# Cross-attention and FP4 FFN on one core: semaphores for the leading stack rows, and another placement of prologue, quantization and late-normalisation work

## The chip, the core and the metric

The kernel runs on one core of a Trainium2 chip. The core has TensorE (PE, with PEld its weight load), VectorE (DVE), ScalarE (ACT), GpSimd (POOL), and SyncE (SP), which here only issues DMAs. An engine's name with a q, as ACTq, is its sequencer, which waits and issues DMAs. The metric is device time in microseconds, the median of several executions; lower is better.

## What is computed

Eight batches of `x` (512 rows of 256) attend to a context of 1601 rows of 256, with 16 heads of 16; then comes a feed-forward part with blockwise FP4 quantization of activations and weights.

```python
x = x + xattn(layernorm(x), ctx, ctx, Wq, bq, Wk, bk, Wv, bv, Wo, bo)
# xattn: softmax(q k^T / 4) v per head, then @ Wo.T + bo
x = x + ffn(layernorm(x), w_gate, w_up, w_down)
# ffn: h = silu(fp4(x) @ fp4(w_gate).T) * (fp4(x) @ fp4(w_up).T); fp4(h) @ fp4(w_down).T
# fp4: per block of 16, scale = max|.|/6, values rounded to the grid 0 .5 1 1.5 2 3 4 6
```

## The kernel before, in words

The kernel is a software pipeline over batches. Iterations are called pre (the prologue), first, six of kind loop, last and tail. In a loop iteration four parts run together: attention of one batch ("att"), the projections of the next ("early"), layernorm and loads of the one after ("next"), and output projection and FFN of the previous one ("late"). The first iteration has no late part, but quantizes and transposes the FFN weights instead ("once"). The last one has no early part.

An iteration has 52 steps: four groups of four heads times 13 tiles of the context. A step does, in this order on TensorE: the scores of two heads (L678), a job from the first list of `SLOTS`, the scores of the other two heads, two products for the row maxima (L692, 26 a group, 18 steps ahead of the scores; in the first steps of the first iteration three), a job from the second list, and the weighted sum of the step before (L707). ScalarE does four exps (L870) and takes most jobs' results; VectorE reduces the products (L941, L943) and runs the pieces of layernorm and quantization that `DVE_EXTRA` and `W_SCALE_AT`, `W_POWER_AT` place behind them; GpSimd does what `POOL_WORK` places. Every engine runs its list in order, and waits in order. Jobs share one bank of PSUM (three in the prologue), so a job waits until its predecessor's result was taken. Products alternate between two buffers.

Queries and keys are split into three bf16 parts, written to DRAM, and read back into `qstack` and `kstack`, whose rows are blocks of parts: 48 leading rows in each half, which the products read, made from two arrangements of the parts. Each half of a group takes six transfers from the queries and six from the keys, and all twelve of a kind count on one semaphore, `q_stack[g]` or `k_stack[g]`. Rows 32 to 63 of the stacks are filled by GpSimd (L1190, L1191) before the transfers: group 0 first, the rest after the first layernorm is ready. Once a group's products are reduced, the negated maxima are transposed (job nm), split on VectorE (L989 to L992) and written by three transfers (L396) as a row of `qstack` that the scores need.

In the prologue, ScalarE issues the query transfers of group 0 (L862), waits for all of them, then loads the other weights. Products of group 0 start at step 34. Job q1 is at step 35, the second half of the keys at 36 to 39, eight v jobs in pairs at 40, 42, 44 and 46. At step 45 TensorE computes the bias that comes from bv and Wo (L735); VectorE adds it to `bob` and clears the bank. At step 47 ScalarE issues the first two raw FFN weight loads (L760).

The weight quantization of one of six pieces: VectorE takes maxima and scales (L1135 to L1137), GpSimd scales (L1249), VectorE makes powers (L1146, L1147), GpSimd rounds in three instructions (L1255 to L1259), and two wT jobs transpose it (L653).

## Time and profile before

| what | value |
|---|---|
| median of 3 runs | 1815.83 us (1815.01 to 1816.35) |
| profiled execution, its own time | 1818.33 us |
| its span, first to last instruction | 1816.5 us |
| PE, DVE, ACT, POOL busy | 1693.3, 1364.4, 1152.6, 522.3 us |
| mean granted TensorE clock | 0.975 |

Spans are cut at the first exp of an iteration or of a step. Instruction groups stand with their line in the kernel, and an arrow `<-` goes from what is written to what is read.

### The profile page before, as it was taken

What the parts mean: (1) busy time and instruction counts of PE and PEld (TensorE: products, weight loads), DVE (VectorE), ACT (ScalarE), POOL (GpSimd) and SP (SyncE); (2) the same over time, 40 slices, a digit from 0 to 9 for tenths busy, and PEclk for the clock granted to TensorE, in tenths of its full rate; (3) what the DMA queues carried; (4) which work ended last, traced back from release to release, by engine and by line L of the source; (5) the groups of instructions that cost most, each with busy time, mean ns of one, the idle gap of its engine ahead of it and who ended that gap; (6) DMA issues with size and microseconds to landing.
All of it is one profiled execution on the core that took longest, in us unless ns stands there. A gap on an engine that the chain in (4) does not pass through costs nothing.

```text
span 1816.5 us, 26586 instructions
## 1 busy us (share of the span) xinstructions
PE 1693.3 (93%) x9600; PEld 662.7 (36%) x9600; DVE 1364.4 (75%) x1970; ACT 1152.6 (63%) x2335; POOL 522.3 (29%) x409
## 2 busy tenths in 40 slices
PE   2699779999999999999999999999999999989978
PEld 2332113433343334433443334433334333323335
DVE  4677778688778877688777887688877887688538
ACT  2167557776667666676667766676667766656651
POOL 4306432153203422062302531054211532012203
PEclk8899889999999999999999999999999999999989
DMA  5544305142240424233060324215051421300000
GB/s 142 143 68 95 59 29 110 19 102 40 75 74 30 88 39 97 36 69 73 25 123 28 75 40 100 48 43 99 19 115 16 102 40 41 60 1 1 10 15 12
DMA packets 98030, 109.08 MB, mean 60 GB/s; under 512 B 18788, under 2 KB 83308, under 8 KB 97900
## 3 DMA queue, kind: packets, MB, share of 16 engines
q1 hardware_dynamic: 93344, 103.26, 27.5%
q10 hardware_dynamic: 4556, 4.13, 0.9%
q8 instruction: 76, 1.25, 0.3%
q14 instruction: 54, 0.44, 0.1%
HBM read 76.78 MB, written 30.16 MB: 59 GB/s over the span
## 4 chain that ended last, share of the span: by engine, by line
PE 75%; DVE 15%; ACT 4%; issue 2%; DMA 1%; POOL 1%; ACTq 0%; SPq 0%; DVEq 0%; POOLq 0%
PE pvb L707 19%; PE st L678 19%; PE mx L692 10%; DVE cmx L941 7%; PE misc L629 7%; PE misc L591 4%; ACT prob L870 3%; PE misc L584 3%; PE misc L646 3%; PE misc L641 2%; PE misc L523 1%; PE misc L608 1%; PE misc L637 1%; PE misc L561 1%; PE misc L572 1%
## 5 line engine op out<-in xcount | busy, mean ns | idle before, releaser
L870 ACT ACTIVATE prob<-st 128x512 f32<-128x512 f32 x1630 | 885.9, 598 | 432.8 <-PE st L678 431.1
L941 DVE TENSOR_REDUCE cmx<-mx 128x2 f32<-128x1024 f32 x768 | 905.9, 1219 | 263.0 <-PE mx L692 259.2
L678 PE MATMUL st<-qstack,kstack 112*128 112x512 bf16 x1630 | 520.9, 388 | 32.5 <-ACT prob L870 17.1
L707 PE MATMUL pvb<-prob,vv 128*17 128x512 f32 (+1 forms) x3328 | 443.4, 605 | 0.6 <-ACT prob L870 0.6
L678 PEld LDWEIGHTS st<-qstack,kstack 112*128 112x128 bf16 x1630 | 128.3, 98 | 552.9 <-issue 293.8
L692 PE MATMUL mx<-kstack,qstack 48*128 48x512 bf16 (+1 forms) x2048 | 253.5, 337 | 43.7 <-DMA qstack<-scr_q 21.3
L1203 POOL TENSOR_TENSOR cin<-cin 128x400 f32<-128x400 f32 (+1 forms) x60 | 55.4, 923 | 374.8 <-ACT cin L798 374.8
L1236 POOL TENSOR_TENSOR ht<-ht,rh 128x704 f32<-128x704 f32 x29 | 40.2, 1388 | 414.6 <-DVE rh L917 414.6
L629 PE MATMUL misc<-wguT,rowsT 128*128 128x352 f32 x456 | 154.3, 460 | 0.0
L692 PEld LDWEIGHTS mx<-kstack,qstack 48*128 48x128 bf16 x2048 | 57.5, 94 | 207.3 <-issue 154.8
L591 PE MATMUL misc<-wv,ctxT 128*128 128x256 f32 (+1 forms) x392 | 102.6, 384 | 0.0
L629 PEld LDWEIGHTS misc<-wguT,rowsT 128*128 128x128 f32 x456 | 86.8, 191 | 40.5 <-issue 0.9
L707 PEld LDWEIGHTS pvb<-prob,vv 128*17 128x17 f32 (+1 forms) x3328 | 55.2, 95 | 116.9 <-issue 95.1
L584 PE MATMUL misc<-ctxT,wk 128*128 128x400 f32 (+1 forms) x240 | 90.8, 500 | 0.0
L591 PEld LDWEIGHTS misc<-wv,ctxT 128*128 128x128 f32 (+1 forms) x392 | 73.7, 188 | 20.5 <-issue 0.5
L1216 POOL TENSOR_TENSOR x<-x,bob 128x1024 f32<-128x1024 f32 x8 | 18.9, 2366 | 193.5 <-DMA x<-x 193.5
L1240 POOL TENSOR_TENSOR ht<-ht,mt 128x704 f32<-128x704 f32 x30 | 50.4, 1680 | 60.2 <-DVE mt L1117 60.2
L1205 POOL TENSOR_TENSOR cin<-cin,one 128x400 bf16<-128x400 f32 (+1 forms) x60 | 57.6, 960 | 4.7
L1207 POOL TENSOR_TENSOR cin<-cin 128x400 bf16<-128x400 f32 (+1 forms) x60 | 55.9, 932 | 4.7
L943 DVE TENSOR_REDUCE cmx<-mx 128x8 f32<-128x520 f32 x64 | 44.4, 693 | 15.6 <-PE mx L692 15.6
L584 PEld LDWEIGHTS misc<-ctxT,wk 128*128 128x128 f32 x240 | 45.4, 190 | 25.0 <-issue 0.7
L973 DVE SCALAR_TENSOR_TENSOR ht<-misc,ht 128x352 f32<-128x352 f32 x57 | 29.7, 520 | 31.9 <-PE misc L629 31.7
(202 smaller groups left out, 1564.5 us busy)
## 6 DMA issues: line engine op xcount, KB each, us to landing
kstack<-scr_k SPq DMA_DIRECT2D x384, 100.1 KB, 4.4
scr_k<-cin SPq DMA_DIRECT2D x48, 300.0 KB, 3.9
qstack<-scr_q SPq DMA_DIRECT2D x372, 32.0 KB, 2.5
cin<-ctx_in SPq DMA_DIRECT2D x8, 1280.0 KB, 7.1
scr_q<-qp SPq DMA_DIRECT2D x15, 384.0 KB, 4.7
scr_k<-cin SPq DMA_DIRECT2D x16, 300.8 KB, 4.5
xn<-x SPq DMA_DIRECT2D x8, 512.0 KB, 4.0
x<-x SPq DMA_DIRECT2D x8, 512.0 KB, 3.8
```

Of the source, the lines that this page charges most:

```text
L584: last = mm(o[:, 0:w], wk[:, h, m * 128:(m + 1) * 128], ctxT[:, h, COFF[n]:COFF[n] + w], start=(h == 0), stop=(h == NC2 - 1))
L591: last = mm(o[0:w, 0:E], ctxT[:, h, KOFF[j]:KOFF[j] + w], wv[:, h, :], start=(h == 0), stop=(h == NC2 - 1))
L629: last = mm(o[:, 0:IH], rowsT[:, h, t * 128:(t + 1) * 128], wguT[:, h, first:first + IH], start=(h == 0), stop=(h == NC2 - 1))
L646: last = mm(o[:, 0:E], hqT[0:FW[f], f, :], wdT[0:FW[f], f, :], start=(f == 0), stop=(f == NF - 1))
L678: mm(score_bank(it, n, pair, h)[0:KROWS[kt], :], kstack[:, hd, KOFF[kt]:KOFF[kt] + KROWS[kt]], qstack[:, hd, :], start=True, stop=True).th ...
L692: last = mm(mx[:, q % 2, par, at:at + w], qstack[r0:r0 + LEAD, hd, t * 128:(t + 1) * 128], kstack[r0:r0 + LEAD, hd, k0:k0 + w], start=True ...
L707: last = mm(pvb[32 * h:32 * h + D + 1, :], vv[0:w, kt, HG * g + h, :], prob[0:w, n % 2, h, :], start=(kt == 0), stop=(kt == NKT - 1))
L870: activate(prob[0:KROWS[kt], n % 2, 2 * pair + h, :], score_bank(it, n, pair, h)[0:KROWS[kt], :], ACT.Exp, scale=SCALE).then_inc(exp_done[ ...
L941: v.tensor_reduce(cmx[:, g % 2, h0:h0 + 2, at:at + 1], products, op=ALU.max, axis=AX.X).then_inc(max_free, 1)
L1203: g_.tensor_tensor(whole, whole, parts[:, 0, :], ALU.subtract).then_inc(step, 1)
L1205: g_.tensor_tensor(parts[:, 1, :], whole, one[:, 0:1].to_broadcast([128, whole.shape[-1]]), ALU.mult).then_inc(step, 1)
L1207: g_.tensor_tensor(parts[:, 2, :], whole, parts[:, 1, :], ALU.subtract).then_inc(done, 1)
```

## The change

The six first transfers of a group, now those with the leading rows of both halves, count on a semaphore of their own; products wait for these, scores for all. In the prologue q1 moves to step 34, keys to 35 to 38, one v job a step from 39 to 46; the fill of the other heads' rows moves behind the first query split, the bias product becomes a job "bob" of the first iteration's step 20, and the raw weight loads move to its step 4. Weight pieces and their transposes get other steps. In the other iterations the second half of the keys is done by step 19, the next context is loaded sooner, gate, up and down jobs shift, and the late normalisation's pieces get steps of their own (the multiplication of `xscale` becomes `xmul`). A down job's first part waits for the first copy of its input alone.

```diff
@@ -83,40 +82,40 @@
     13: ([("k", 3, "early")], []),
     14: ([("k", 4, "early")], []),
     15: ([("q", 1, "early")], []),
-    16: ([("pvT", 0, "att")], [("xqT", 0, "late")]),
-    17: ([("k", 5, "early")], [("xqT", 1, "late")]),
-    18: ([("k", 6, "early")], []),
-    19: ([("gate", 0, "late")], []),
-    20: ([("gate", 1, "late")], []),
-    21: ([("up", 0, "late")], [("nm", 2, "att")]),
-    22: ([("up", 1, "late"), ("wT", 0, "once")], []),
-    23: ([("gate", 2, "late"), ("wT", 1, "once")], []),
-    24: ([("gate", 3, "late"), ("wT", 2, "once")], []),
-    25: ([("up", 2, "late"), ("wT", 3, "once")], []),
-    26: ([("up", 3, "late")], [("hqT", 0, "late")]),
-    27: ([("gate", 4, "late")], [("hqT", 1, "late")]),
-    28: ([("down0", 0, "late")], []),
-    29: ([("down", 0, "late")], [("pvT", 1, "att")]),
-    30: ([("gate", 5, "late")], []),
-    31: ([("up", 4, "late"), ("wT", 4, "once")], [("hqT", 2, "late")]),
-    32: ([("up", 5, "late"), ("wT", 5, "once")], [("hqT", 3, "late")]),
-    33: ([("gate", 6, "late"), ("wT", 6, "once")], []),
-    34: ([("down0", 1, "late")], []),
-    35: ([("down", 1, "late")], [("nm", 3, "att")]),
-    36: ([("gate", 7, "late"), ("wT", 7, "once")], []),
-    37: ([("up", 6, "late")], [("hqT", 4, "late")]),
-    38: ([("up", 7, "late")], [("hqT", 5, "late")]),
-    39: ([("down0", 2, "late")], []),
-    40: ([("down", 2, "late"), ("wT", 8, "once")], []),
-    41: ([("k", 7, "early")], []),
-    42: ([("v", 0, "early")], [("pvT", 2, "att")]),
-    43: ([("v", 1, "early")], [("hqT", 6, "late"), ("wT", 9, "once")]),
-    44: ([("v", 2, "early")], [("hqT", 7, "late")]),
-    45: ([("down0", 3, "late"), ("wT", 10, "once")], []),
-    46: ([("down", 3, "late"), ("wT", 11, "once")], []),
+    16: ([("k", 5, "early")], []),
+    17: ([("k", 6, "early")], []),
+    18: ([("pvT", 0, "att")], [("xqT", 0, "late")]),
+    19: ([("k", 7, "early")], [("xqT", 1, "late")]),
+    20: ([("gate", 0, "late"), ("bob", 0, "once")], []),
+    21: ([("gate", 1, "late")], [("nm", 2, "att")]),
+    22: ([("up", 0, "late")], []),
+    23: ([("up", 1, "late")], []),
+    24: ([("gate", 2, "late"), ("wT", 0, "once")], []),
+    25: ([("gate", 3, "late"), ("wT", 1, "once")], []),
+    26: ([("up", 2, "late")], []),
+    27: ([("up", 3, "late"), ("wT", 2, "once")], [("hqT", 0, "late")]),
+    28: ([("gate", 4, "late"), ("wT", 3, "once")], [("hqT", 1, "late")]),
+    29: ([("down0", 0, "late")], []),
+    30: ([("down", 0, "late")], []),
+    31: ([("gate", 5, "late")], [("pvT", 1, "att")]),
+    32: ([("up", 4, "late")], [("hqT", 2, "late")]),
+    33: ([("up", 5, "late")], [("hqT", 3, "late")]),
+    34: ([("gate", 6, "late"), ("wT", 4, "once")], [("nm", 3, "att")]),
+    35: ([("down0", 1, "late"), ("wT", 5, "once")], []),
+    36: ([("down", 1, "late")], []),
+    37: ([("gate", 7, "late"), ("wT", 6, "once")], [("hqT", 4, "late")]),
+    38: ([("up", 6, "late"), ("wT", 7, "once")], [("hqT", 5, "late")]),
+    39: ([("up", 7, "late")], []),
+    40: ([("down0", 2, "late")], []),
+    41: ([("down", 2, "late")], [("pvT", 2, "att")]),
+    42: ([("v", 0, "early")], []),
+    43: ([("v", 1, "early")], [("hqT", 6, "late"), ("wT", 8, "once")]),
+    44: ([("v", 2, "early")], [("hqT", 7, "late"), ("wT", 9, "once")]),
+    45: ([("down0", 3, "late")], []),
+    46: ([("down", 3, "late")], []),
     47: ([("v", 3, "early")], [("nm", 0, "early")]),
-    48: ([("v", 4, "early")], []),
-    49: ([("v", 5, "early")], []),
+    48: ([("v", 4, "early")], [("wT", 10, "once")]),
+    49: ([("v", 5, "early")], [("wT", 11, "once")]),
     50: ([("v", 6, "early")], []),
     51: ([("v", 7, "early")], []),
...
-    35: ([("q", 1, "early")], []),
-    36: ([("k", 4, "early")], []), 37: ([("k", 5, "early")], []), 38: ([("k", 6, "early")], []), 39: ([("k", 7, "early")], []),
-    40: ([("v", 0, "early"), ("v", 1, "early")], []), 42: ([("v", 2, "early"), ("v", 3, "early")], []),
-    44: ([("v", 4, "early"), ("v", 5, "early")], []), 46: ([("v", 6, "early"), ("v", 7, "early")], []),
+    34: ([("q", 1, "early")], []),
+    **{35 + j: ([("k", 4 + j, "early")], []) for j in range(4)}, **{39 + j: ([("v", j, "early")], []) for j in range(8)},
...
 DVE_EXTRA = {
-    1: [("late", "norm", 3)], 5: [("late", "stats", 0)], 6: [("late", "stats", 1)], 7: [("late", "mean", 0)],
-    9: [("late", "root", 0)], 10: [("att", "nm", 1), ("late", "apply", 0)], 11: [("late", "apply", 1), ("late", "xmax", 0)],
-    12: [("late", "xscale", 0)], 13: [("late", "xpower", 0)], 15: [("late", "xlast", 0)], 16: [("att", "norm", 0)],
-    21: [("att", "nm", 2)], 22: [("late", "hscale", 0)], 23: [("late", "hpower", 0)], 26: [("late", "hscale", 1)], 27: [("late", "hpower", 1)],
-    29: [("att", "norm", 1)], 32: [("late", "hscale", 2)], 33: [("late", "hpower", 2)], 35: [("att", "nm", 3)], 38: [("late", "hscale", 3)], 39: [("late", "hpower", 3)],
-    42: [("att", "norm", 2), ("next", "stats", 0)], 43: [("next", "stats", 1)], 45: [("next", "mean", 0)], 46: [("next", "root", 0)],
+    1: [("late", "norm", 3)], 5: [("late", "stats", 0)], 6: [("late", "stats", 1)], 7: [("late", "mean", 0)], 8: [("late", "root", 0)],
+    9: [("late", "apply", 0)], 10: [("att", "nm", 1)], 11: [("late", "apply", 1)], 12: [("late", "xmax", 0)], 13: [("late", "xscale", 0)],
+    14: [("late", "xmul", 0)], 15: [("late", "xpower", 0)], 17: [("late", "xlast", 0)], 19: [("att", "norm", 0)],
+    21: [("att", "nm", 2)], 23: [("late", "hscale", 0)], 24: [("late", "hpower", 0)], 27: [("late", "hscale", 1)], 28: [("late", "hpower", 1)],
+    31: [("att", "norm", 1)], 33: [("late", "hscale", 2)], 34: [("late", "hpower", 2)], 35: [("att", "nm", 3)], 39: [("late", "hscale", 3)], 40: [("late", "hpower", 3)],
+    42: [("att", "norm", 2)], 43: [("next", "stats", 0)], 44: [("next", "stats", 1)], 45: [("next", "mean", 0)], 46: [("next", "root", 0)],
     47: [("early", "nm", 0)], 49: [("next", "apply", 0)], 50: [("next", "apply", 1)],
...
-W_SCALE_AT = {17: 0, 18: 1, 26: 2, 29: 3, 35: 4, 39: 5}
-W_POWER_AT = {19: 0, 21: 1, 28: 2, 30: 3, 37: 4, 41: 5}
+W_SCALE_AT = {17: 0, 19: 1, 28: 2, 31: 3, 38: 4, 41: 5}
+W_POWER_AT = {20: 0, 22: 1, 30: 2, 33: 3, 40: 4, 43: 5}
...
-    14: [("late", "xround", 0), ("early", "k", 3)], 15: [("early", "k", 4)], 16: [("early", "q", 1)], 18: [("early", "k", 5)], 19: [("early", "k", 6)],
-    23: [("late", "hscaled", 0)], 24: [("late", "hround", 0)], 27: [("late", "hscaled", 1)], 28: [("late", "hround", 1)],
-    33: [("late", "hscaled", 2)], 34: [("late", "hround", 2)], 39: [("late", "hscaled", 3)], 40: [("late", "hround", 3)], 42: [("early", "k", 7)],
+    14: [("early", "k", 3)], 15: [("early", "k", 4)], 16: [("early", "q", 1), ("late", "xround", 0)], 17: [("early", "k", 5)], 18: [("early", "k", 6)], 20: [("early", "k", 7)],
+    24: [("late", "hscaled", 0)], 25: [("late", "hround", 0)], 28: [("late", "hscaled", 1)], 29: [("late", "hround", 1)],
+    34: [("late", "hscaled", 2)], 35: [("late", "hround", 2)], 40: [("late", "hscaled", 3)], 41: [("late", "hround", 3)],
...
+        k_stack = [[sem(f"k_stack{g}_{n}") for n in ("lead", "rest")] for g in range(NG)]
+        q_stack = [[sem(f"q_stack{g}_{n}") for n in ("lead", "rest")] for g in range(NG)]
...
                 src = scr_q.rearrange("(h i) a n -> i h a n", i=D)
-                for half in range(2):
+                for rest in range(2):
                     for par in range(2):
-                        for j, a in enumerate(Q_PARTS[half ^ par]):
-                            row = HALF * half + D * j
-                            sp.dma_start(qstack[row:row + D, HG * g + par:HG * (g + 1):2, :], src[:, HG * g + par:HG * (g + 1):2, a, :]).then_inc(q_stack[g], 16)
...
 
-                sp.wait_ge(q_stack[0], STACK)
-                sp.wait_ge(k_stack[0], STACK)
+                sp.wait_ge(q_stack[0][0], BLOCKS)
+                sp.wait_ge(k_stack[0][0], BLOCKS)
...
                     queries_in(it, 0, "early")
                     keys_in(it, 0, "early")
+                    keys_out(it, 1, range(1))
                     queries_out(it, 1)
-                    keys_out(it, 1, range(3))
+                    keys_out(it, 1, range(1, 4))
                 if has_att:
                     maxima_in(it, 2, "att")
+                if has_next:
+                    ctx_in_rows(it, "next")
                 if has_early:
                     queries_in(it, 1, "early")
                     keys_in(it, 1, "early")
@@ -495,16 +498,11 @@
                     rows_out(it, 1)
                 if has_next:
                     x_in(it, "next")
-                if has_late:
-                    rows_out(it, 2)
-                if has_early:
-                    keys_out(it, 1, range(3, 4))
-                if has_next:
-                    ctx_in_rows(it, "next")
                 if has_early:
                     queries_in(it, 2, "early")
                     keys_in(it, 2, "early")
                 if has_late:
+                    rows_out(it, 2)
                     rows_out(it, 3)
                 if has_att:
...
+                    elif kind == "bob":
+
+                        pe.wait_ge(bvl_ready, 1)
+                        for h in range(NC2):
+                            last = mm(o[:, 0:E], bvl[:, h, :], wo[:, h, :], start=(h == 0), stop=(h == NC2 - 1))
...
                             last = turn(o[0:FW[f], n * 128:(n + 1) * 128], ht[:, t, f * 128:f * 128 + FW[f]], ident[:, :])
                     elif kind == "down0":
-                        pe.wait_ge(free["hqT"], c(2 * QT, 2 * j + 2))
+                        pe.wait_ge(free["hqT"], c(2 * QT, 2 * j + 1))
                         for f in range(NF // 2):
                             mm(o[:, 0:E], hqT[0:FW[f], f, :], wdT[0:FW[f], f, :], start=(f == 0), stop=False)
                         return
                     elif kind == "down":
-                        pe.wait_ge(free["hqT"], c(2 * QT, 2 * j + 2))
+                        if it.kind == "tail":
+                            pe.wait_ge(free["hqT"], c(2 * QT, 2 * j + 1))
                         for f in range(0 if it.kind == "tail" else NF // 2, NF):
+                            if f == (4 if it.kind == "tail" else NF // 2):
+                                pe.wait_ge(free["hqT"], c(2 * QT, 2 * j + 2))
                             last = mm(o[:, 0:E], hqT[0:FW[f], f, :], wdT[0:FW[f], f, :], start=(f == 0), stop=(f == NF - 1))
                     else:
                         p, half = divmod(j, 2)
...
-                        pe.wait_ge(k_stack[g], it.count(part, STACK, STACK))
-                        pe.wait_ge(q_stack[g], it.count(part, STACK, STACK))
+                        pe.wait_ge(k_stack[g][0], it.count(part, BLOCKS, BLOCKS))
+                        pe.wait_ge(q_stack[g][0], it.count(part, BLOCKS, BLOCKS))
                     need(pe, max_free, it.count(part, M_BATCH, q - 1))
...
-                    if it.kind == "pre" and n == BIAS_AT:
-                        pe.wait_ge(s_ones, 2)
-                        pe.wait_ge(bvl_ready, 1)
-                        for c in range(NC2):
-                            last = mm(pvb[:, 0:E], bvl[:, c, :], wo[:, c, :], start=(c == 0), stop=(c == NC2 - 1))
-                        last.then_inc(bo_full, 1)
-
...
                         first_queries()
-                        act.wait_ge(q_stack[0], STACK)
-                        act.wait_ge(k_stack[0], STACK)
+                        act.wait_ge(q_stack[0][1], BLOCKS)
+                        act.wait_ge(k_stack[0][1], BLOCKS)
                         weights_in()
-                    if it.kind == "pre" and n == 47:
+                    if it.kind == "first" and n == 4:
                         raw_in(0)
                         raw_in(1)
                     if has_att:
...
                         link(below(rx[:, :]), part)
+                    elif what == "xmul":
                         link(v.tensor_tensor(blocks(xa[:, :]), blocks(xa[:, :]), over(rx[:, :]), ALU.mult), part)
...
 
-            for heads, done in ((slice(0, HG), 4), (slice(HG, H), 6)):
-                if done == 6:
-                    pool.wait_ge(xn_ready, 1)
+            def fill(heads, done):
+
                 g_.memset(kstack[32:64, heads, :].bitcast(F32), 1.0 + 2.0 ** -23 * 0x3F80).then_inc(c_link, 1)
                 g_.memset(qstack[32:64, heads, :].bitcast(F32), 0.0).then_inc(c_link, 1)
                 pool.wait_ge(c_link, done)
+
+            fill(slice(0, HG), 4)
 
             def bias_columns():
...
-                    if it.kind == "pre" and n == BIAS_AT:
+                    if it.kind == "pre" and n == 15:
+                        pool.wait_ge(q_split, 1)
+                        fill(slice(HG, H), 6)
+                    if it.kind == "first" and n == 6:
                         bias_columns()
```

Left out: the removed names, the same renaming of `half` to `rest` in `keys_in` and in ScalarE's `first_queries`, and the take of "bob" on VectorE, which adds the product into `bob` and signals `free["bob"]`, which GpSimd's bias step waits for.

## Rows read from the trace of the kernel before

**Rows 1.** The page, part 1: busy us (share of the span) xinstructions.
```profile
PE 1693.3 (93%) x9600; PEld 662.7 (36%) x9600; DVE 1364.4 (75%) x1970; ACT 1152.6 (63%) x2335; POOL 522.3 (29%) x409
```

**Rows 2.** The windows, by iteration: us, then PE, PEld, DVE, ACT, POOL busy, clock.
```profile
0.00:92.44 92.44, 44.44 (x177) 24.49 (x178) 50.89 (x98) 20.19 (x40) 33.24 (x31) 0.80 0.59 141
92.44:313.70 221.26, 192.67 (x1080) 59.87 (x1080) 171.61 (x201) 137.38 (x277) 77.54 (x55) 0.93 0.36 71
313.70:522.42 208.72, 205.79 (x1196) 80.93 (x1195) 163.30 (x237) 143.25 (x291) 60.86 (x50) 1.00 0.30 63
1566.83:1751.14 184.31, 174.94 (x1010) 61.23 (x1008) 115.08 (x171) 124.86 (x252) 31.60 (x19) 0.98 0.08 14
```

**Rows 3.** The windows, single steps and runs of steps, in order.
```profile
216.58:220.05 3.47, 2.84 (x17) 0.55 (x16) 2.79 (x4) 2.16 (x4) 1.49 (x1) 1.00 1.04 136
175.98:206.12 30.14, 20.18 (x101) 4.90 (x101) 23.84 (x23) 12.03 (x25) 18.88 (x11) 0.77 0.10 33
227.59:245.53 17.94, 11.45 (x67) 3.03 (x66) 13.95 (x15) 7.47 (x15) 9.99 (x5) 0.85 0.07 21
256.33:267.07 10.74, 8.39 (x33) 1.38 (x32) 8.78 (x11) 4.32 (x8) 4.28 (x4) 0.70 0.15 52
153.30:156.96 3.66, 3.66 (x27) 1.20 (x26) 2.23 (x3) 3.15 (x7) 2.46 (x4) 1.00 0.30 98
790.42:795.17 4.75, 3.90 (x28) 1.38 (x27) 4.68 (x6) 3.15 (x7) 0.44 (x1) 1.00 0.04 16
1619.77:1625.54 5.77, 4.85 (x23) 0.84 (x22) 5.62 (x7) 2.17 (x6) 1.74 (x1) 0.50 0.01 1
850.53:855.21 4.68, 4.68 (x28) 1.95 (x27) 3.37 (x4) 2.62 (x6) 1.96 (x2) 1.00 0.19 41
```

**Rows 4.** The chain of waits in the prologue: start us, us, what.
```profile
39.88 5.52 DMA qstack<-scr_q
...
46.58 3.18 PE st L572 x4
...
69.47 1.86 PE st L591 x4
...
86.38 5.23 DMA qstack<-nmp
```

**Rows 5.** The timeline, all engines, first key split.
```profile
11.75 8.10 POOL L1190 MEMSET kstack<- 32x9612 f32 x1 [6.53 <-DVE xn L1035]
...
19.60 0.58 DVE L1123 TENSOR_TENSOR cin<-cin 128x401 f32<-128x401 f32 x1 [7.97 <-ACT cin L798]
19.80 2.65 POOL L1191 MEMSET qstack<- 32x3072 f32 x1
...
20.21 2.47 DVE L1125 CAST cin<-cin 128x401 bf16<-128x401 f32 x1
...
23.81 0.37 DVE L1125 CAST cin<-cin 128x400 bf16<-128x400 f32 x1
```

**Rows 6.** The DMA issues from 37.0 to 37.3: KB each, us to landing.
```profile
qstack<-scr_q ACTq DMA_DIRECT2D x2, 32.0 KB, 7.2
```

**Rows 7.** The DMA issues of the whole span, same columns.
```profile
qstack<-nmp SPq DMA_DIRECT2D x96, 4.0 KB, 1.7
```

**Rows 8.** The timeline, first and last reductions, raw weight loads.
```profile
46.19 1.23 DVE L941 TENSOR_REDUCE cmx<-mx 128x2 f32<-128x1024 f32 x1 [11.82 <-PE mx L692]
...
82.91 0.22 DVE L947 TENSOR_REDUCE nmx<-cmx 128x16 f32<-128x64 f32 x1
...
83.69 0.90 ACTq L760 DMA_DIRECT2D ht<-w_gate  x2
```

**Rows 9.** The timeline, split of the maxima at step 21, first iteration.
```profile
190.31 2.34 POOL L1255 TENSOR_TENSOR ht<-ht,mt 88x1024 f32<-88x1024 f32 x1 [1.60 <-DVE mt L1147]
190.39 2.40 DVE L990 TENSOR_TENSOR nmr<-nmf,nmp 16x128 f32<-16x128 f32 x1
```

**Rows 10.** The timeline, TensorE, last down job of the tail.
```profile
1810.91 2.40 PE L646 MATMUL mx<-wdT,hqT 128*128 128x256 f32 x10 [0.86 <-ACT hqT L834]
```

More of the change, by code:

```diff
@@ L857, in first_queries @@
                     src = scr_q.rearrange("(h i) a n -> i h a n", i=D)
[L858 removed]
+                    for rest in range(2):
                         for par in range(2):
[L860 to L862 removed]
+                            for j, a in enumerate(Q_PARTS[rest]):
+                                row = HALF * (par ^ rest) + D * j
+                                act.dma_start(qstack[row:row + D, par:HG:2, :], src[:, par:HG:2, a, :]).then_inc(q_stack[0][rest], 16)
                 def exps(n, pair):
@@ L951, in take @@
                     kind, j, part = job
-                    if kind not in ("o", "gate", "up", "down"):
+                    if kind not in ("o", "gate", "up", "down", "bob"):
                         return
@@ L957, in c @@
                         return it.count(part, per, k)
-                    dve.wait_ge(full[kind], job_count(it, job))
-                    if kind == "o":
+                    dve.wait_ge(full[kind], 1 if part == "once" else job_count(it, job))
+                    if kind == "bob":
+                        v.tensor_tensor(bob[:, :], bob[:, :], src[:, 0:E], ALU.add).then_inc(free["bob"], 1)
+                    elif kind == "o":
                         if j == 0:
```

48 lines of the change are left out of this document (21 added, 27 removed).

## The prediction, made before the changed kernel ran

> **What bounds the kernel now.** I read the busy shares, cut the span into iterations, cut the iterations into steps, then followed the chain of waits where a cut was longer than its neighbours. TensorE is busy 93% of the span [rows 1], but that mixes stages. The six loop iterations take 208.7 us each at full granted clock, TensorE busy 205.8 of them: nearly tight. The prologue before the first exp takes 92.4 us with TensorE busy 44.4. The first iteration takes 221.3 with 192.7 busy, though it has no FFN work [rows 2]. So the slack is in those two.
>
> The step is the unit. A step with no projection job takes 3.47 us, TensorE only 2.84 busy [rows 3]: scores, exp, scores, exp, two products, weighted sum. One job between the two halves of the scores hides under the exps (a v step also takes 3.47); the excess, and any job behind the products, adds to it. VectorE must reduce two products a step, 2.27 us, and the products have two buffers: an extra of up to 2.4 us behind the reductions costs nothing, what exceeds it holds TensorE.
>
> Where steps exceed this: steps 20 to 24 of the first iteration take 30.1 us against 17.6 (4 at 3.47, one at 3.68 with a transpose); steps 31 to 33 take 17.9 against 10.4; steps 37 and 38 take 10.7 against 6.9 [rows 3]: 12.5 + 7.5 + 3.8 = 23.8 us lost around the weight quantization. Step 14 takes 4.75 in a loop iteration but 3.66 in the first, which has no late normalisation; in the last iteration it takes 5.77, at a granted clock of 0.50 [rows 3].
>
> **Prologue, until the first reduction.** The chain passes a VectorE cast of 2.47 us that shares its interval with the GpSimd fill of the stack; the same cast takes 0.37 for the next piece [rows 5]. The fill of the other heads moves behind the first query split, so the first key split ends 2.1 us earlier. Keys out and their stack transfers move by about 2.0; the query's split and write follow ScalarE's third and fourth key pieces, which wait for that split, and move by 1.9 until their own product holds them. Products then wait for stack rows: now for all twelve query transfers, the last of which lands at 39.88 + 5.52 = 45.40 [rows 4]. With the lead semaphore they wait for six. The sixth is issued at 37.03 and takes some 7.2 us [rows 6], so 44.1; less 1.9 to 2.0, 42.1. **Term: 3.3 us.**
>
> The moved fill takes 8.10 + 2.65 us [rows 5], from 29.2 to 40, over VectorE's layernorm of the next batch, and SyncE waits for it before it issues group 1. Both are needed only at 42, so it costs nothing; without that cover, SyncE's wait would delay group 1. A two-input VectorE operation ran its normal 0.58 us under the first fill [rows 5]. The Trainium skill (SBUF — State Buffer, section "SBUF: two separate sides") says two SBUF inputs are held only against a GpSimd operation that reads SBUF, while a two-port mode is held by any; this row agrees, and by that rule the layernorm is free at 32.5. If each small operation were held, it would end at 42.7: 0.6 us worse.
>
> **Prologue, the reductions.** The first starts at 46.19, the last work on them ends at 82.91 + 0.22: 36.9 us [rows 8]. Pure VectorE work is 24 x 1.135 + 2 x 0.65 = 28.5. The rest comes from q1 between the first products (3.18 us at low clock), v jobs in pairs (1.86 and 1.71 at low clock), and the bias product [rows 4]. Now q1 runs before the stack arrives, each step has one job, and the bias is out. I keep 1.4 us for the first key job at low clock, 0.7 for the next, 0.9 for turnarounds: 31.5. **Term: 5.4 us**; bounds 8.4 (VectorE alone) and 2 (only bias and q1 gain).
>
> **Prologue, the row of maxima.** The last of its three transfers lands 5.23 us after issue [rows 4]; the median over the kernel is 1.7 [rows 7]. Two raw weight loads of 352 KB are issued at 83.69, just ahead [rows 8]. They move to step 4 of the first iteration. I take 1.9: **3.3 us**, bounds 0 and 3.6. GpSimd's splits end near 62, keys land at 65, so the next context's load is done near 73, ahead of the row at 76. The first exp moves 12.0 us earlier, to about 80.4.
>
> **First iteration.** VectorE from step 19: reductions 2.27, norm 0.7, scales 2.2; then the bias add 0.42, 2.27, powers 1.4 plus 1.1 of contention; then 2.1, the split of the maxima 1.0 plus contention; then 2.27. That split is the dear one: beside GpSimd's rounding a 0.28 us subtraction took 2.40, as long as GpSimd's 2.34 us instruction [rows 9]. It now starts 2.2 us into a rounding of 6.6, so it is held 4.4 us. Sum 20.1 us over four steps of 14.5: 5.6 lost instead of 12.5, **gain 6.9**. At 31, scale and norm still meet the rounding begun at 30, as they now do at 29: about 4.3 lost, plus 1.4 for low clock; the wait at 33 for a piece to be transposed goes: **gain 1.8**. The last pieces have pauses of two steps: 1 lost of 3.8, **gain 2.8**. Against it: four transposes go behind the products where one was, **+1.6**; two raw loads on ScalarE's queue, **+0.7**. Net 9.2; bounds 3 (contention persists) and 16.
>
> **Loop iterations.** Late apply, maximum, scale, multiply and power get a step each, and no extra is over 2.4 us, so step 14 falls to the first iteration's 3.66 and step 15 rises 0.1: -1.0. The rest is a permutation of the same jobs: a last down job paired with a transpose costs 4.68 where 3.86 + 0.59 would do [rows 3]. Pairing transposes with gate jobs, which are released only after tanh and multiply, costs some 0.15 each; down 2 with a transpose, 0.2; the pairs undone give most of it back: +0.3. Net 0.65 a loop, **4 us in six**; bounds -9 and +4. SyncE now issues the next context's load some 20 steps earlier, behind key pieces written near step 21: hidden, since the next thing behind it is needed near step 26 or later. GpSimd's late rounding now follows q1 and ends near 1.2 us before VectorE asks for it.
>
> **Last iteration and tail.** Steps 11, 13 and 14 return to 3.4 to 3.5: 3.3 us; one gate job moves past step 33, where no product hides it: +1.0. Net **2.3**. In the tail, down jobs wait for both copies of their input, 0.86 us, the last at 1810.91 [rows 10]; with half the wait, 0.35 each for two on the path: **0.7**. Bias and weights-in are otherwise unchanged.
>
> **Sum.** 12.0 + 9.2 + 4 + 2.3 + 0.7 = 28.2 us. The profiled execution took 1818.33 us: 1790.1. The median of the runs is 2.5 us below it: 1787.6, say 1788.
>
> **Rivals.** (a) *Low clock in the prologue.* If TensorE stays at 1.2 GHz through the v jobs (granted 0.5 made them 1.86 us), each step is 1.86 + 0.9 against 2.27, and key jobs 3.6: 6 us more, 1794. For: the clock did fall there. Against: one v a step, without pairs, leaves fewer gaps. (b) *Contention moves but stays.* VectorE and GpSimd do the same quantization work; if the held operations just change names, the first iteration gives 3 or less, 1794 to 1798. For: each rounding is still 6.6 us beside small VectorE operations. Against: the waits for GpSimd itself do go. (c) *Loops gain more.* If late reductions also caused what pairs of jobs cost now, each loop gives 2 us: 1780 or below. (d) *Slower.* GpSimd's late rounding sits behind q1's split, and VectorE waits for it in order, the reductions behind it. It gives slower only if it ends over 7 us later than I place it: 1.2 + 1.2 of slack, then 4.7 us a loop to eat the whole gain; 1825 at 8.5 late. For: one GpSimd operation is stretched by contention now and then. Against: its queue has some 2 us of room a step. (e) *The change doesn't do what it says* at the first products: SyncE or ScalarE could still hold them to the last rows; then 1.3 less, inside the range.
>
> **Chances.** Forecast within 6 us either way 0.5; (a) or (b) or both 0.27, 1794 to 1803; (c) 0.17, 1773 to 1782; (d) 0.03; something unseen 0.03. The range takes in (a), (b) and most of (c): 1775 to 1802. Measurement of this kernel tells about 0.2%, 3.6 us. Faster by more 0.95, within 0.01, slower 0.04.
>
> **What would show it.** First products near 42; 26 reductions without gaps of 2 us, ending near 74; row of maxima landing 2 us after issue; first exp near 80. In the first iteration steps 20 to 24 near 23 to 24 us, step 31 or 33 still long, 37 and 38 at 3.5. Loop iterations near 208.0, with step 14 at 3.7. Wrong it would be if loops moved by over 1.5 us each, or if steps 19 to 23 lost as much as 20 to 24 do now.

## The result, and the profile after

The changed kernel takes 1802.26 us, the median of 4 runs (1801.16 to 1803.74), where the kernel before took 1816.09 beside it (1815.01 to 1821.07). The ratio is 0.9923, its 95% interval 0.9908 to 0.9938: faster by 0.8%, half of the 28 us that I forecast, and just above the range. The profiled execution took 1801.16 us, its span is 1799.4. The page's part 1, against [rows 1]:

```profile
PE 1687.2 (94%) x9600; PEld 658.4 (37%) x9600; DVE 1398.6 (78%) x1969; ACT 1155.4 (64%) x2335; POOL 528.4 (29%) x409
```

VectorE is busy 34 us longer for the same instructions: some of them are held. The windows by iteration, against [rows 2]: prologue, first iteration, first loop iteration, last iteration to the first exp of its step 51. (The window of [rows 2] for the last iteration ends 3.2 us behind that exp, so these two lines don't compare; the table below cuts both alike.)

```profile
0.00:78.74 78.74, 40.84 (x173) 21.31 (x174) 56.30 (x96) 19.90 (x39) 32.98 (x31) 0.85 0.64 154
78.74:291.25 212.51, 190.17 (x1084) 60.72 (x1084) 169.57 (x202) 137.65 (x278) 77.12 (x55) 0.95 0.39 78
291.25:501.66 210.41, 206.52 (x1196) 80.97 (x1195) 168.28 (x237) 143.62 (x290) 61.85 (x49) 1.00 0.30 63
1551.75:1733.00 181.25, 170.54 (x993) 60.45 (x991) 119.75 (x171) 123.41 (x249) 31.56 (x19) 1.00 0.08 15
```

| stretch | before | after | difference | forecast |
|---|---|---|---|---|
| prologue, to the first exp | 92.44 | 78.74 | -13.7 | -12.0 |
| first iteration | 221.26 | 212.51 | -8.8 | -9.2 |
| six loop iterations | 1253.13 | 1260.50 | +7.4 | -4 |
| last iteration, to its step 51 | 181.09 | 181.17 | +0.1 | -2.3 |
| tail, from there to the end | 68.61 | 66.44 | -2.2 | -0.7 |

So the loops have the wrong sign, and are 11 us off; the prologue and the first iteration hold; the last two lines are near the forecast only together. These stretches are those of the two profiled executions, which are 17.2 us apart where the medians are 13.8 apart. The six loop iterations take 210.41, 210.32, 209.87, 210.38, 209.86 and 209.66 us.

The steps of [rows 3] in the windows after: 20 to 24, 31 to 33 and 37 to 38 of the first iteration; step 14 of the first loop iteration and of the last; then steps 31 and 49 of the first loop iteration, which before took 4.27 and 3.47.

```profile
162.94:188.31 25.37, 19.98 (x97) 4.75 (x97) 23.59 (x27) 11.36 (x22) 16.93 (x11) 0.80 0.28 90
209.36:225.75 16.39, 10.65 (x59) 2.56 (x59) 16.15 (x18) 6.96 (x15) 8.57 (x4) 0.80 0.00 1
236.37:243.33 6.96, 6.33 (x41) 1.84 (x39) 4.71 (x5) 4.83 (x10) 0.00 (x0) 1.00 0.48 140
350.58:354.24 3.66, 3.66 (x27) 1.20 (x26) 3.13 (x6) 3.16 (x7) 2.52 (x4) 1.00 0.28 93
1604.22:1607.61 3.39, 2.62 (x22) 0.65 (x22) 3.18 (x6) 2.18 (x5) 0.00 (x0) 1.00 0.03 7
418.25:422.79 4.54, 4.33 (x26) 1.73 (x25) 3.41 (x4) 2.98 (x8) 0.00 (x0) 1.00 0.00 0
490.02:494.70 4.68, 3.71 (x22) 1.39 (x21) 4.61 (x7) 2.39 (x6) 0.00 (x0) 1.00 0.02 3
```

Step 14 is what I said it would be. Step 49 isn't: TensorE is busy 3.71 of 4.68 us and VectorE 4.61. The timeline of VectorE, GpSimd and the products ahead of it shows why:

```profile
487.27 2.37 POOL L1215 TENSOR_TENSOR x<-x,bob 128x1024 f32<-128x1024 f32 x1 [21.71 <-DMA x<-x]
487.42 2.29 DVE L991 CAST nmp<-nmf 16x128 bf16<-16x128 f32 x1
...
490.51 4.60 DVE L941 TENSOR_REDUCE cmx<-mx 128x2 f32<-128x1024 f32 x4
...
492.91 0.39 PE L699 MATMUL mx<-kstack,qstack 48*128 48x512 bf16 x2 [0.74 <-DVE cmx L941]
```

GpSimd's bias add (L1215), released by the residual rows' DMA, starts just before the first cast of the split of the maxima (L991), whose median over the kernel is 0.205 us; the cast ends with it, the reductions behind it are late, and TensorE waits. The trace of before has the same meeting, in its last loop iteration alone, which takes 209.58 us where its neighbours take 208.71:

```profile
1552.43 2.37 POOL L1216 TENSOR_TENSOR x<-x,bob 128x1024 f32<-128x1024 f32 x1 [22.08 <-DMA x<-x]
1552.54 2.34 DVE L989 CAST nmp<-nmf 16x128 bf16<-16x128 f32 x1
```

I had read one loop iteration of six. What let the add come early is in SyncE's queue: the load of the residual rows (L445) waits until the output rows (L441) have landed. Before, in its second loop iteration, 24 stack transfers stand ahead of those, and the output rows land 5.9 us after their issue:

```profile
700.48 6.12 SPq L425 DMA_DIRECT2D qstack<-scr_q  x12
706.78 5.44 SPq L436 DMA_DIRECT2D kstack<-scr_k  x12
712.26 0.42 SPq L441 DMA_DIRECT2D out<-x  x1
718.23 0.39 SPq L445 DMA_DIRECT2D x<-x  x1
```

After, the keys are done sooner, nothing stands just ahead, the output rows land in 2.4 us, and the load is issued 0.6 us into step 47 rather than 4.7:

```profile
481.04 0.36 SPq L441 DMA_DIRECT2D out<-x  x1
483.48 0.39 SPq L445 DMA_DIRECT2D x<-x  x1
```

Over the six loops the load is issued 2.6, 4.7, 3.0, 4.9, 3.0 and 0.3 us into step 47 before, and from 0.2 us ahead of it to 0.6 into it after: 2 to 5 us sooner in the first five.

The second loss is in step 31, a gate job (L632) with a transpose (L601, job pvT) behind the products. The timeline of one such step of after:

```profile
419.59 0.47 ACT L824 ACTIVATE xn<-misc 128x352 f32<-128x352 f32 x1 [0.26 <-PE misc L632]
420.15 0.52 DVE L970 SCALAR_TENSOR_TENSOR ht<-xn,misc 128x352 f32<-128x352 f32 x1 [1.13 <-ACT xn L824]
420.73 0.42 PEld L601 LDWEIGHTS misc<-ident,pvs 128*128 128x128 f32 x4 [0.70 <-DVE ht L970]
```

The transpose needs the bank that tanh and then VectorE's multiplication free. Before had one such pair (gate 4 with hqT1), after has five.

### The profile page after: what moved, and what is told of

Same layout as the page of the kernel before. It is cut to its first block, busy times and chain, and to the rows that moved or that the text cites. A ratio compares the mean times of both kernels' runs of the same rounds, so it can differ in the third digit from the quotient of the medians.

```text
span 1799.4 us, 26659 instructions
## 1 busy us (share of the span) xinstructions
PE 1687.2 (94%) x9600; PEld 658.4 (37%) x9600; DVE 1398.6 (78%) x1969; ACT 1155.4 (64%) x2335; POOL 528.4 (29%) x409
## 4 chain that ended last, share of the span: by engine, by line
PE 74%; DVE 15%; ACT 7%; issue 3%; DMA 1%; ACTq 0%; POOL 0%; SPq 0%; DVEq 0%; POOLq 0%
PE pvb L714 19%; PE st L685 18%; PE mx L699 9%; PE misc L632 7%; DVE cmx L941 6%; PE misc L582 5%; ACT prob L870 4%; PE misc L589 4%; PE misc L644 2%; PE misc L652 2%; PE misc L521 1%; PE misc L640 1%; PE misc L611 1%; PE misc L570 1%; PE misc L559 1%
## 5 line engine op out<-in xcount | busy, mean ns | idle before, releaser
L632 PE MATMUL misc<-wguT,rowsT 128*128 128x352 f32 x456 | 154.9, 462 | 0.0
L632 PEld LDWEIGHTS misc<-wguT,rowsT 128*128 128x128 f32 x456 | 87.1, 191 | 41.4 <-issue 1.0
L1206 POOL TENSOR_TENSOR cin<-cin 128x400 bf16<-128x400 f32 (+1 forms) x60 | 60.7, 1011 | 4.7
L1215 POOL TENSOR_TENSOR x<-x,bob 128x1024 f32<-128x1024 f32 x8 | 18.9, 2362 | 145.2 <-DMA x<-x 145.2
```

What stands on the lines that cost most here:

```text
L632: last = mm(o[:, 0:IH], rowsT[:, h, t * 128:(t + 1) * 128], wguT[:, h, first:first + IH], start=(h == 0), stop=(h == NC2 - 1))
L1206: g_.tensor_tensor(parts[:, 2, :], whole, parts[:, 1, :], ALU.subtract).then_inc(done, 1)
```

## The experiments

Eleven kernels, each timed against the kernel before in one of three batches, so that ratios compare best. "Loop" is the mean of the six loop iterations, from the first exps of the trace.

| kernel | median us | ratio to before, 95% | first exp | first iteration | loop |
|---|---|---|---|---|---|
| before | 1816.1 to 1817.5 | | 92.44 | 221.26 | 208.86 |
| after | 1802.26 | 0.9908 to 0.9938 | 78.74 | 212.51 | 210.08 |
| e1_bias_wait | 1798.59 | 0.9876 to 0.9920 | 79.05 | 215.84 | 209.18 |
| e2_pairs | 1793.99 | 0.9852 to 0.9900 | 79.25 | 212.27 | 208.86 |
| e3_sync_order | 1800.76 | 0.9894 to 0.9933 | 80.70 | 213.35 | 209.56 |
| e4_late_alone | 1813.30 | 0.9973 to 0.9994 | 93.08 | 221.43 | 208.72 |
| e5_prologue | 1804.32 | 0.9915 to 0.9950 | 79.79 | 221.77 | 208.78 |
| e6_old_quant | 1811.58 | 0.9962 to 0.9982 | 78.82 | 220.51 | 210.07 |
| e7_both | 1788.98 | 0.9835 to 0.9865 | 78.80 | 212.37 | 208.08 |
| e8_quant_apart | 1785.66 | 0.9817 to 0.9850 | 78.22 | 205.42 | 208.64 |
| e9_quant_spaced | 1778.04 | 0.9769 to 0.9802 | 78.78 | 205.04 | 208.08 |
| e10_old_late | 1823.07 | 1.0019 to 1.0045 | 78.81 | 212.43 | 212.68 |
| e11_down_waits | 1803.86 | 0.9920 to 0.9950 | 79.53 | 212.43 | 210.05 |

**The bias add, held** (e1_bias_wait, from after).

```diff
                         pool.wait_ge(free["bob"], 1)
+                        if "att" in it.parts:
+                            pool.wait_ge(nmp_ready, it.count("att", NG, 1))
```

> After's kernel (median 1802.3 us, first exps of the loop iterations 210.1 us apart on the mean), with GpSimd's bias add made to wait for the split of group 0's maxima, so that it can't lie over it. Theory A (the residual rows arrive some 4 us sooner because the output rows are no longer queued behind stack transfers; the add therefore meets the split at step 48, VectorE's first cast takes 2.3 us in place of 0.3, and TensorE waits in step 49): step 49 falls from 4.1-4.7 to about 3.5 us, the cast to about 0.3, a loop iteration by 0.7 to 1.2, the whole by 4 to 6 us, to 1796-1798. Theory B (the loops lose only to the way jobs are paired): the cast is shorter, but the loop iteration stays within 0.3 of 210.1 and the whole within 2 us of 1802.3.

Step 49 went to 3.47 us in all six loops, the cast to 0.20; a loop fell by 0.90. Theory A holds for this part. The whole fell by 3.7 only: in this execution the first iteration was 3.3 us longer, 1.9 of it in steps 0 and 1, which nothing of the edit touches (see the last section for those), and 1.4 in steps 21 to 24 and 34, around the weight quantization.

**SyncE's queue as before** (e3_sync_order, from after).

```diff
-                    keys_out(it, 1, range(1))
                     queries_out(it, 1)
-                    keys_out(it, 1, range(1, 4))
+                    keys_out(it, 1, range(3))
 ...
-                if has_next:
-                    ctx_in_rows(it, "next")
 ...
+                if has_late:
+                    rows_out(it, 2)
+                if has_early:
+                    keys_out(it, 1, range(3, 4))
+                if has_next:
+                    ctx_in_rows(it, "next")
```

> After's kernel with SyncE's queue in the order of before (the next context's rows behind output rows 1 and 2, the last key piece of heads 4 to 7 behind output rows 2, keys before queries); all else as after. Theory A: the residual rows land as late as before, the bias add falls behind the split again, and step 49 is back at about 3.5: 0.7 to 1.2 us a loop iteration, 1796-1798, as in the run with the bias add held. Rival (the order of the queue costs by itself, as traffic or as late rows): more than that, under 209.0 a loop iteration. Theory B: no change, 210.1 an iteration, 1802.

Half of it. In the first three loops the add starts 6.90, 6.84 and 5.57 us after step 47's first exp, behind the split (4.56), and step 49 takes 3.47; in the next three it starts at 5.30, 3.94 and 3.66, and step 49 takes 4.77, 4.22 and 3.94. So the queue's order shifts the add, but doesn't fix its place. At 5.30 the split's first cast (4.56, 0.20 us) escaped and step 49 was longest: the add fell on the rest of the split.

**Transposes away from gate jobs** (e2_pairs, from after).

```diff
-    21: ([("gate", 1, "late")], [("nm", 2, "att")]),
-    22: ([("up", 0, "late")], []),
+    21: ([("up", 0, "late")], [("nm", 2, "att")]),
+    22: ([("gate", 1, "late")], []),
 ...
-    31: ([("gate", 5, "late")], [("pvT", 1, "att")]),
+    30: ([("down", 0, "late")], [("pvT", 1, "att")]),
 ...
-    34: (gate 6, nm 3)    37: (gate 7, hqT 4)    38: (up 6, hqT 5)
+    36: (down 1, nm 3)    38: (up 6, hqT 4)      39: (up 7, hqT 5)
```

The last two lines are shortened. The jobs nm, pvT and hqT are transposes; with nm 3, VectorE's split of group 3's maxima goes from step 35 to 36.

> After's kernel with four transposes taken off the steps whose first job is a gate job (nm2 behind up0, pvT1 behind down 0, nm3 behind down 1, hqT4 behind up6; one gate pair is left). Theory B (a job behind a gate job costs some 0.27 us more, for VectorE frees the bank only after tanh): steps 21, 31, 34 and 37 together lose about 1.1 us a loop iteration beyond what their new partners gain in theirs; an iteration near 209.0, the whole 6 us less, near 1796. Theory A (the loops lose at the split of the maxima): iterations within 0.4 of 210.1, the whole within 3 us of 1802.3, and step 49 stays over 4.1.

A loop fell by 1.22 us, to 208.86, and the whole by 8.3. Step by step the loops read: nm2 4.16 to 3.89 in step 21; pvT1 0.86 over its gate job alone (4.59 against 3.73), 0.59 over the down job (4.68 against 4.09); nm3 0.48 against 0.21. That is 0.27 for each pair, and the fourth, hqT4, gives the same over steps 37 to 39. Step 49 stayed at 4.28, so this cause is separate.

**Both** (e7_both: the two edits above together).

> After's kernel with both causes found taken out: the bias add held behind the split of the maxima, and the four transposes away from gate jobs. They cost 0.85 and 1.2 us a loop iteration by themselves. If they are separate causes: 210.1 - 2.05 = 208.05 a loop iteration, step 49 at 3.47, the whole near 1789 to 1791. Rival (they share a cause, so that only one of the gains is had): 208.9 or more an iteration, the whole 1793 or more.

208.08 us, and 1788.98: the causes add up. And 208.08 is 0.78 under before's 208.86, where I had forecast 0.65: what the change does in the loops is what I said, plus two losses that I had not priced.

**The late normalisation alone** (e4_late_alone, from before; the edit shortened).

```diff
-    9: [root], 10: [nm 1, apply 0], 11: [apply 1, xmax], 12: [xscale], 13: [xpower], 15: [xlast], 16: [norm 0]
+    8: [root], 9: [apply 0, apply 1], 10: [nm 1], 11: [xmax], 12: [xscale], 13: [xmul], 14: [xpower], 16: [norm 0, xlast]
-    16: (pvT 0, xqT 0)  17: (k 5, xqT 1)    GpSimd 14: xround, k 3
+    17: (k 5, xqT 0)    18: (k 6, xqT 1)    GpSimd 15: k 4, xround
```

> Before's kernel (median 1816.1, loop iterations 208.7 us apart) with only the late normalisation spread: root at step 8, both applies at 9, maximum 11, scale 12, multiply 13, powers 14, GpSimd's rounding behind the key split of step 15, last multiply at 16, the two transposes of its result at 17 and 18. My reckoning of the change's gain in steps 11 to 15: step 14 falls by 1.1 us in a loop iteration and by some 2.3 in the last, nothing else moves: 207.6 a loop iteration, the whole 1816.1 - 6.6 - 2.3 = 1807. Rival (the stall moves to another step, as GpSimd's rounding is then the wait): 208.7 an iteration and 1814-1816.

Step 14 fell by 1.09 in each loop and from 5.77 to 3.39 in the last iteration, as reckoned; but steps 16 to 18 rose from 12.84 to 13.72, 5.55 of it in step 17. There TensorE's transpose waits 1.08 us for VectorE's last multiplication, which stands behind group 0's normalisation in one step and takes 2.06 us beside a GpSimd split (1.44 before, where the transpose waits 0.21). Net 0.14 a loop: the rival was mostly right for this placing, though the wait is for VectorE and not for the rounding.

**The late normalisation bunched again** (e10_old_late, from after; the edit shortened).

```diff
-    8: [root], 9: [apply 0], 10: [nm 1], 11: [apply 1], 12: [xmax], 13: [xscale], 14: [xmul], 15: [xpower]
+    9: [root], 10: [nm 1, apply 0], 11: [apply 1, xmax], 12: [xscale, xmul], 13: [xpower]
```

> After's kernel with the late normalisation's pieces put together again in steps 9 to 13 as before (root 9, first apply with group 1's split 10, second apply and maximum 11, scale and multiply 12, powers 13). My reckoning: spreading them is what took 1.1 us out of step 14 of every loop iteration and 2.9 out of steps 13 and 14 of the last: step 14 back at 4.75, a loop iteration 211.2, the whole 1802.3 + 6.6 + 2.9 = 1812. Rival (with rounding behind q1's split in GpSimd's queue anyway, the bunch no longer meets it): loops under 210.5, the whole under 1806.

Twice my figure: a loop took 212.68, 2.6 more, 2.2 of it in step 14 (5.90), and the kernel became slower than before. The timeline of its step 13 and 14:

```profile
350.29 1.89 DVE L1049 TENSOR_TENSOR xa<-xa,rx 128x1024 f32<-128x1024 f32 x1
351.18 1.75 POOL L1206 TENSOR_TENSOR cin<-cin 128x400 bf16<-128x400 f32 x1
352.21 2.36 DVE L941 TENSOR_REDUCE cmx<-mx 128x2 f32<-128x1024 f32 x2
...
355.52 1.33 DVE L1052 TENSOR_SCALAR mt<-mt 128x1024 f32<-128x1024 f32 x1
```

With the rounding moved behind the keys in GpSimd's queue, key splits run beside the multiplication and the powers (1.89 and 1.33 us; 1.22 and 0.69 in before's trace at the same work), and each holds the other: GpSimd's split instruction takes 1.75 where it takes 0.95 alone. In after the same three VectorE operations are held as long (1.59, 1.07 and 1.53 us, together 4.2 as here), but each has a step to itself: the spreading doesn't end the meeting, it hides it. Steps 14 and 15 together take 8.96 us before, 8.01 after and 10.67 here. So the spreading is worth 2.7 us there in this kernel, the other moves had used up 1.7, and neither is the 1.0 that I wrote.

**The prologue alone** (e5_prologue: before, with semaphores, one job a step, fill, bias job and raw loads of after).

> Before's kernel with only the parts of the change that touch the prologue: leading rows with semaphores of their own, one projection job a prologue step, the second fill behind the first query split, the bias product as a job of step 20 of the first iteration, the raw weights loaded from its step 4. After's trace puts the first exp 13.7 us sooner. If that gain is the prologue's alone: first exp near 78.7 to 79.5, everything behind it as before, 1816.1 - 13.5 = about 1802.5. Rival (part of it is given back in the first iteration, where the raw loads and the bias product now lie, or at the collision of the bias add): first iteration over 222.3 us or loops over 208.9, the whole 1804 or more.

First exp 12.7 us sooner, the first iteration 0.5 longer (with 1.9 in steps 0 and 1, see the last section), the loops as before, the last iteration 1.1 shorter in its step 14; 11.8 off the median. So of the change's 13.8 us the prologue has about 12; all its other parts together gave 2.

**The old steps for the weights** (e6_old_quant, from after).

```diff
-W_SCALE_AT = {17: 0, 19: 1, 28: 2, 31: 3, 38: 4, 41: 5}
-W_POWER_AT = {20: 0, 22: 1, 30: 2, 33: 3, 40: 4, 43: 5}
+W_SCALE_AT = {17: 0, 18: 1, 26: 2, 29: 3, 35: 4, 39: 5}
+W_POWER_AT = {19: 0, 21: 1, 28: 2, 30: 3, 37: 4, 41: 5}
```

> After's kernel with the weight quantization's steps and its transposes' slots of before; the key jobs, normalisation of group 0 and all else as after. My term for the first iteration was 11.5 us gained by the new spacing, less 2.3 for slots and loads. If the spacing is what gained it: steps 20 to 24 back near 30, 31 to 33 near 18, 37 and 38 near 10.5, first iteration near 221, the whole near 1810. Rival (the key job and the normalisation moved away from steps 17 and 18 are what gained it): first iteration under 217, the whole under 1806. Loops as after, 210.1, in both.

Steps 20 to 24 took 31.0, 31 to 33 15.7, 37 and 38 11.9; the first iteration 220.5, the whole 9.3 more. The spacing gains 8.0 of the 8.8 us by which the first iteration is shorter; all else in it gains 0.8.

**Down jobs waiting for both copies** (e11_down_waits, from after).

> After's kernel with down jobs waiting for both copies of their input again. My reckoning of the half wait was 0.7 us in the tail and nothing elsewhere: the stretch from the last step to the end 0.6 to 0.8 us longer, the rest as after, the whole 1803. Rival (the half wait also opened TensorE's loads in down steps of loops): steps 29, 30, 35, 36, 40 and 41 longer by 0.1 or more each, the whole 1806. If nothing changes, the term was nothing.

No step of the loops moved. In the tail the wait before a down job is 0.87 us here and 0.55 in after: 0.32 each. The rest of the 1.9 us by which the tail differs lies where the other kernels' tails differ too (66.4 to 70.2 us over all runs, with a granted clock of 0.66 to 0.80 in its first 25), so the whole doesn't show this term.

**Weights apart from small operations** (e8_quant_apart, from e7_both).

```diff
+W_SCALE_AT = {17: 0, 23: 1, 27: 2, 32: 3, 37: 4, 41: 5}
+W_POWER_AT = {18: 0, 24: 1, 28: 2, 33: 3, 38: 4, 42: 5}
+    22: [("att", "nm", 2), ("att", "norm", 0)],   # wT at 22, 23, 27, 28, 31, 32, 37, 38, 41, 45, 46
```

> The last kernel, with weight quantization placed so that GpSimd rounds (6.6 us from the step after a piece's powers) only in steps where VectorE has nothing small to do: scales at steps 17, 23, 27, 32, 37, 41, powers one step later, the split of group 2's maxima and group 0's normalisation together at 22, the weight transposes in steps 22, 23, 27, 28, 31, 32, 37, 38, 41, 45 and 46 ahead of the second scores. Theory (VectorE's small operations are held to the end of GpSimd's instruction, and that is all that is left in steps 21 to 33): the excess of 13.8 us that after's first iteration still shows there falls to 4 or less, and 1.3 us of transposes behind products is saved: first iteration 201 to 204, loops as in the last kernel, the whole near 1780. Rival (the excess is VectorE's own work, or GpSimd's time for a piece): first iteration over 208, the whole over 1785.

Steps 21 to 24 lost nothing now (6.52, 5.19, 6.80, 3.49 in after became 3.68, 3.47, 3.47, 3.49) and step 33 fell from 8.85 to 3.65: VectorE's small operations, held, were all that was left there. But step 27 took 7.05, for its transpose asked for a piece still being rounded, and the split at 22 made the row of maxima 0.55 us late for step 26 in every iteration. First iteration 205.4.

**And the waits that this left** (e9_quant_spaced, from e8_quant_apart).

```diff
+W_SCALE_AT = {16: 0, ...    W_POWER_AT = {17: 0, ...
+    21: [("att", "nm", 2)], 22: [("att", "norm", 0)],   45: [("att", "norm", 2), ("next", "mean", 0)]
+    wT 2 at 28, wT 3 at 29, wT 11 at 50
```

> The kernel with quantization set apart (first iteration 205.4, loops 208.6), with the four waits that its trace still shows taken out: piece 0 a step earlier (scale 16, powers 17), so that its rounding ends before the key pieces and the split of group 2's maxima, which goes back to step 21; its row then lands before the scores of step 26 ask for it (0.55 us in every iteration); transposes of pieces two and three at 28 and 29, four steps behind the powers, where step 27 took 7.05 us waiting for the rounding; group 2's normalisation at 45, behind the last rounding; the last transpose at 50. If each wait was what it seems: steps 20, 25, 27, 44, 46 lose 0.9, 0.55, 3.6, 1.0 and 0.6: first iteration near 199, loops back at 208.1, the whole 1773 to 1777. Rival (the waits move on to the next step with a small operation): first iteration over 202, the whole over 1779.

Steps 20, 27, 44 and 46 lost what was said or a little more, step 25 0.4 (0.55 in the loops, which are back at 208.08). But the first iteration took 205.04 us, not 199, which is what the rival said of it: against the kernel above, step 31 took 2.0 us more, steps 19 and 50 0.6 and 0.8, steps 38 to 40 3.2. In step 31 (6.40) the next transpose is three steps behind its powers rather than four. TensorE's wait there, and the window behind it:

```profile
204.89 0.49 PE L659 MATMUL misc<-ident,ht 88*128 88x88 f32 x4 [1.94 <-POOL ht L1260]
```

```profile
206.00:210.00 4.00, 3.89 (x19) 0.90 (x15) 2.94 (x4) 1.64 (x4) 0.00 (x0) 0.60 0.00 0
```

After that wait of 1.9 us the granted clock is 0.60 for 4 us. In steps 38 to 40 TensorE waits 0.80 us for group 3's row of maxima, whose third transfer is issued 2.2 us behind the first (1.2 in e8_quant_apart, where TensorE doesn't wait for it); the granted clock over these steps is 0.75, against 1.00 there. Why that issue came late stays open. The other three executions took 1776.4 to 1778.5, against 1781.15 for the profiled one. At 1778 the kernel is 2.1% faster than before, and 24 us faster than after.

## Why the prediction was half right

**Prologue, forecast 12.0, measured 13.7 in the trace and 12.7 alone.** The first products came at 42.0 (forecast 42.1), the reductions ran from 42.66 to 72.93, 30.3 us (31.5), and the granted clock stayed at 1.00 from 46 to 70, through the v jobs, where rival (a) feared for it. The three terms of 3.3, 5.4 and 3.3 measured 3.5, 6.7 and 3.5. The three transfers of the row of maxima took 1.87 us to issue, and the last landed 1.75 after its issue (forecast 1.9):

```profile
74.89 1.87 SPq L394 DMA_DIRECT2D qstack<-nmp  x3
...
78.12 1.01 PE L685 MATMUL st<-qstack,kstack 112*128 112x512 bf16 x2 [4.67 <-DMA qstack<-nmp]
```

One cover was thinner than I wrote. I had the layernorm under the fill free at 32.5. It ended at 40.65:

```profile
30.60 0.16 DVE L1034 SCALAR_TENSOR_TENSOR rs<-tmp,rs 128x4 f32<-128x4 f32 x1
30.80 9.85 DVE L1037 TENSOR_SCALAR xn<-xn,mv,rs 128x256 f32<-128x256 f32 x4
```

The operations with two inputs ran at 0.16 us under the fill; the four with one input took 6.47, 2.82, 0.40 and 0.40, the first two ending 0.15 us behind the fill's two instructions. It cost nothing, for the first product was at 42. By the Trainium skill (SBUF — State Buffer, "SBUF: two separate sides") a two-port mode is held by any GpSimd operation for its whole instruction and two-input operations only by one that reads SBUF. The trace agrees on the second half, and on the first if these four ran in such a mode, which the trace doesn't name; I had applied the second half to an operation with one input.

**First iteration, forecast 9.2, measured 8.8.** Right in size, in part by luck: within it the terms are off in both directions. Steps 20 to 24 gained 4.8 of a forecast 6.9, for the split of the maxima met the rounding as before (2.46 and 1.91 us at two instructions); 31 to 33 gained 1.6 (1.8), the stall being in 33 as scale and norm were held; 37 and 38 gained 3.8 (2.8); all other steps together lost 1.35 (2.3). The spacing is the cause, as the run with the old steps shows. Rival (b) was right about the place, wrong about the amount.

**Loops, forecast -4, measured +7.4: the step that failed.** It lies outside even the term's bounds, -9 and +4. The step is the sentence that the rest is a permutation of the same jobs, which I priced at +0.3 a loop; with it goes "hidden" for SyncE's moved load. Three things in it:
- "Pairing transposes with gate jobs costs some 0.15 each", given back by the pairs undone: it costs 0.27 each, four times net, 1.1 to 1.2 us a loop, and nothing came back. I had priced a down job alone at 3.86, a step of small products; alone it takes 4.09, and 4.09 + 0.59 is the 4.68 of [rows 3]. Those pairs had no stall to give.
- I asked of the queue behind SyncE's moved load only what would come later. What came sooner was the residual, by 2 to 5 us, and with it a GpSimd instruction onto the split: 0.90 us a loop with it held back.
- The gain of 1.0 a loop in steps 14 and 15 was seen in after (0.95), but by luck in part: it is the rest of two larger terms, 2.7 gained and 1.7 spent.

With the first two undone a loop takes 208.08, 0.78 under before. My own sign of being wrong, loops that move by over 1.5 us each, was set too wide: 1.2 us was enough. The loops account for the 11.1 us by which the profiled execution (1801.16) missed its forecast of 1790.1. The median missed by 3.6 us more, because I took 2.5 us off for going from the profiled execution to the median, and after's median is 1.1 above its profiled execution.

**Last iteration and tail, forecast 3.0, measured 2.1: luck.** The last iteration, forecast 2.3 shorter, is 0.1 longer. Its steps 13 and 14 gave 2.9 (4.10 and 5.77 to 3.61 and 3.39), and the other steps took all of it back, where I had allowed 1.0; taking four transposes off the gate jobs (e2_pairs) gives 1.9 of it back. The tail is 2.2 shorter, forecast 0.7. The half wait is 0.32 each, as reckoned; the rest is within what tails differ by from kernel to kernel, and stays open.

**Rival (d)**, GpSimd's late rounding as a new wait, did not happen. That another small GpSimd instruction would meet another small VectorE one was not among the rivals; it is rival (b)'s mechanism in a stretch where I had not looked.

## What to carry to other kernels

When a change lets a queue run earlier, list what arrives sooner, not only what arrives later, and what each arrival triggers on GpSimd; then look in every iteration of the old trace for the one where that meeting already happens. Price a pair of jobs by the same job alone in a neighbouring step, not by the cheapest step that has it, and ask which engine frees the bank between the two. Between VectorE's small operations and GpSimd's long ones, keep a step free: here that was worth 7 us in 52 steps, and a transpose had to stand four steps behind the powers, not three.

## What the chip showed that I had not expected

- The meeting works by order of arrival, and it costs the smaller operation the rest of the larger one: the same 16x128 cast took 0.20 us in most iterations and 1.74 to 2.29 in after's six loops, where the bias add (2.37 us) had started 0.7 to 0.15 us before it; the longer before, the shorter the cast. VectorE's maxima of 88x1024 from SBUF took 1.21 us with or without GpSimd beside them; powers of a weight piece took 0.68 and 0.69 alone and 1.2 each beside key splits.
- Steps 0 and 1 of the first iteration took 5.56 and 3.99 us in most executions and 6.08 and 5.38 in two, e1_bias_wait and e5_prologue, with no wait in them. The granted clock in the latter is still 0.54 where after has 1.00:

```profile
84.00:88.00 4.00, 3.88 (x23) 1.44 (x22) 3.56 (x4) 2.45 (x5) 0.00 (x0) 1.00 0.99 177
```

```profile
85.00:89.00 4.00, 4.00 (x14) 1.89 (x12) 1.80 (x2) 2.40 (x6) 0.00 (x0) 0.54 0.96 172
```

  The first is after's window, the second that of the kernel with the prologue alone. TensorE had waited 4.7 us for the row of maxima just before the first exp in both. What decides how soon the clock comes back stays open; it makes 1.9 us between executions, more than several terms that were disputed here.
